# Two transformer layers on one core: score and maximum matmuls issued in runs of four heads, with all other TensorE work behind each run

## What is computed

```
x = x + xattn0(layernorm(x), ctx)      # causal self-attention ("s") plus cross-attention ("x"), added, one projection
x = x + ffn0(layernorm(x))             # 256 -> 1024 -> 256, ternary weights, 8-bit tokens, gelu
x = x + xattn1(layernorm(x), ctx, ctx) # cross-attention ("f")
x = x + ffn1(layernorm(x))             # 8-bit with one scale for the whole tensor: needs a maximum over all batches
```

## Time and profile before

| | us |
|---|---|
| median of 3 runs | 1773.9 (1767.2 to 1776.56) |
| profiled execution | 1771.38 |
| its span, first to last instruction | 1769.6 |
| from the first score of the first unit to the start of the last unit, 95 units | 58.6 to 1643.5 |
| PE busy | 1542.9 (87%) |
| DVE, ACT, POOL busy | 1331.3 (75%), 1141.1 (64%), 464.1 (26%) |
| mean granted TensorE clock | 0.932 of full speed |

### The profile page before, as it was taken

How to read it: one execution, slowest core, us unless ns; L and a number is a source line. 1 busy time by engine, 2 the same in 40 slices (tenths; PEclk the granted TensorE clock), 3 DMA queues, 4 the chain that set the end, 5 groups by cost and what they waited for, 6 DMA issues and landing times.

```text
span 1769.6 us, 31233 instructions
## 1 busy us (share of the span) xinstructions
PE 1542.9 (87%) x11094; PEld 664.2 (38%) x11094; DVE 1331.3 (75%) x2583; ACT 1141.1 (64%) x2178; POOL 464.1 (26%) x677
## 2 busy tenths in 40 slices
PE   3998889988999989988998899988988987898677
PEld 1244334423443235423542344323543442232226
DVE  6787765888678777888688876888488687778287
ACT  1374575667856675676765685667655854866497
POOL 3211412330324122331333132422341232310130
PEclk9798979999999989999999999999999898789899
DMA  6322201212121212121121212121221121011313
GB/s 185 98 85 85 87 19 34 73 46 67 34 73 49 70 40 67 53 62 57 34 74 41 63 47 67 52 70 56 56 63 33 29 64 31 25 59 39 143 60 120
DMA packets 115018, 110.99 MB, mean 63 GB/s; under 512 B 21552, under 2 KB 108720, under 8 KB 114864
## 3 DMA queue, kind: packets, MB, share of 16 engines
q1 hardware_dynamic: 114864, 108.99, 20.8%
HBM read 69.35 MB, written 38.80 MB: 61 GB/s over the span
## 4 chain that ended last, share of the span: by engine, by line
PE 52%; DVE 23%; ACT 12%; issue 4%; POOL 4%; DMA 3%; SPq 2%; ACTq 0%; POOLq 0%; DVEq 0%
PE acc L1628 13%; DVE nmax L1367 12%; PE st L1614 10%; PE misc L1558 8%; PE misc L1530 5%; ACT probs L1048 4%; PE misc L1584 4%; PE misc L1655 3%; PE misc L1570 3%; ACT tail_h L1118 2%; DVE hid L1316 2%; PE misc L1595 2%; PE misc L1682 2%; DMA stack<-nrow 2%; ACT tail_h L1103 1%
## 5 line engine op out<-in xcount | busy, mean ns | idle before, releaser
L1367 DVE TENSOR_REDUCE nmax<-misc 128x1 f32<-128x512 f32 (+3 forms) x1408 | 863.5, 660 | 261.4 <-PE misc L1584 128.7
L1048 ACT ACTIVATE probs<-st 128x512 f32<-128x512 f32 (+3 forms) x1536 | 756.1, 546 | 323.8 <-PE st L1614 205.4
L1584 PE MATMUL misc<-stack 48*128 48x512 f16 (+3 forms) x1536 | 484.0, 372 | 45.2 <-DVE nmax L1367 37.5
L1614 PE MATMUL st<-stack 50*128 50x512 f16 (+3 forms) x1536 | 472.9, 372 | 56.3 <-ACT probs L1048 43.8
L1614 PEld LDWEIGHTS st<-stack 50*128 50x128 f16 x1536 | 119.4, 94 | 503.2 <-ACT probs L1048 294.0
L1584 PEld LDWEIGHTS misc<-stack 48*128 48x128 f16 x1536 | 129.1, 94 | 117.2 <-DVE nmax L1367 86.8
L1628 PE MATMUL acc<-probs,v_x 128*32 128x512 f32 x1152 | 172.8, 675 | 0.0
L927 POOL TENSOR_TENSOR parts<-qk,zero 128x512 f16<-128x512 f32 x78 | 81.1, 1040 | 295.4 <-ACT qk L1034 295.3
L1034 ACT ACTIVATE qk<-misc,b 128x512 f32<-128x512 f32 x96 | 66.0, 687 | 137.6 <-PE misc L1558 137.3
L1628 PE MATMUL acc<-probs,v_s 128*32 128x512 f32 (+3 forms) x1152 | 115.8, 474 | 0.1
L1628 PE MATMUL acc<-probs,v_f 128*32 128x512 f32 x768 | 107.3, 632 | 0.0
(11 more groups left out here) (282 smaller groups left out, 2088.7 us busy)
## 6 DMA issues: line engine op xcount, KB each, us to landing
parts_xk<-parts SPq DMA_DIRECT2D x36, 128.0 KB
parts_xq<-parts SPq DMA_DIRECT2D x36, 128.0 KB
stack<-parts_xq SPq DMA_DIRECT2D x72, 64.0 KB, 2.1
stack<-parts_xk SPq DMA_DIRECT2D x72, 64.0 KB, 2.0
xn_A<-in_x_dram SPq DMA_DIRECT2D x8, 512.0 KB, 4.4
hid<-in_L_ffn_w_dram SPq DMA_DIRECT2D x4, 1024.0 KB, 5.4
parts_sk<-parts SPq DMA_DIRECT2D x32, 128.0 KB
parts_sq<-parts SPq DMA_DIRECT2D x32, 128.0 KB
```

Source lines behind the costliest of these rows:

```text
L1048: act.activation(probs[:, j % P_SLOTS, c, T - w:], st_bank(n, 4 * j + c)[:, 0:w], ACT.Exp, scale=scale_of[s.unit[1]]).then_inc(exp_done, 1)
L1367: dve.tensor_reduce(nmax[:, ring, first:first + NT * (len(cs) - 1) + 1:NT], src, AX.X, ALU.max, negate=True).then_inc(misc_free[slot], 1)
L1584: last = pe.matmul(o, stack[rows, r, 0, c // 2, P * i:P * i + P], stack[rows, r, 1, c // 2, 0:w], start=True, stop=not causal)
L1614: last = pe.matmul(o[:, 0:w], stack[rows, r, 1, c // 2, P * j:P * j + P], stack[rows, r, 0, c // 2, T - w:T], start=True, stop=not causal)
```

## The change

A constant `RUN = 4` groups the places. Since a block has four heads, each block becomes one run: the four pairs follow one another, then `values` (and in block 0 `heads_copy`), then `heads_out` (block 1), `negmax_T` (block 2) or `negmax` (block 0), and then the other steps of all four places in one piece. No instruction is added or removed, and buffers, banks and semaphores are as before. Only the order in the list differs.

```diff
+RUN = 4
     for j in range(NT):
-        for c in range(HU):
-            out.append(("scores", u, j, c))
-            out += maxima[HU * j + c]
-            if c == 3 and j:
+        for c in range(0, HU, RUN):
+            for d in range(c, c + RUN):
+                out.append(("scores", u, j, d))
+                out += maxima[HU * j + d]
+            last_run = c + RUN == HU
+            if last_run and j:
                 out.append(("values", u, j - 1))
-            if (j, c) == (0, 3) and prev:
+            if last_run and j == 0 and prev:
                 out += [("values", prev, NT - 1), ("heads_copy", prev)]
-            if (j, c) == (1, 1) and prev:
+            if c == 0 and j == 1 and prev:
                 out.append(("heads_out", prev))
-            if (j, c) == (0, 2) and next_:
+            if c == 0 and j == 2 and next_:
+                out.append(("negmax_T", next_))
+            if last_run and j == 0 and next_:
                 out.append(("negmax", next_))
-            if (j, c) == (2, 0) and next_:
-                out.append(("negmax_T", next_))
-            out += others[HU * j + c]
+            for d in range(c, c + RUN):
+                out += others[HU * j + d]
```

## The result

| | before | after |
|---|---|---|
| median of 4 runs, us | 1775.23 (1767.2 to 1778.37) | 1897.81 (1894.36 to 1905.75) |
| profiled execution, us | 1771.38 | 1905.75 |
| its span, us | 1769.6 | 1903.9 |
| mean granted TensorE clock | 0.932 | 0.891 |

The ratio is 1.0688 [1.0656, 1.072]: the kernel is slower, by 122.6 us where 49 were forecast, and the time lies 12 us above the stated range (1749 to 1886). Lines are five higher than before (L1614 is now L1619, L1584 is L1589, L1602 is L1607).

The account below looks back on a forecast made before the run. PE's order was taken to bound most stretches (52% of the chain, DVE 23%). Terms -52 + 85 + 10 + 10 + 10 = +63 us, times 0.77 = 49, turned 1771.4 into 1820 us; eight in ten, 1749 to 1886.

Parts of the forecast that it names:

- The faster rival: Fourth score's wait falls where PE would wait for DVE or ACT anyway: 1749 us, chance 0.17.
- The fourth score's wait: Fourth score waits for ACT's exp to free a bank: 0.45 us in 150 full-width blocks, 0.2 in 91 others, +85 us.
- Copies out late: ACT's copies from the block's last step delay the next run's first exp: +10 us, bounds 0 and 20.
- The next unit's maxima: `negmax_T` comes 2.1 us later, its DMA delaying the next unit's first score: +10 us, bounds 0 and 76.
- maxima late in most tight units: Rival: SP is free, so 2.1 us come through in all 36 cases, +76 instead of +10: 1886 us, chance 0.15.
- No clock term: TensorE clock given no cost, since it stayed at 1.00 in a stretch full of such waits.
- the factor 0.77: DVE has 23% of the chain, where a later PE costs nothing: 63 x 0.77 = 49 us.
- the prediction's own sum before the factor: All five terms where PE sets the pace: -52 + 85 + 10 + 10 + 10 = +63 us.
- the 52 us: Net gain on PE: 71 us of removed switches less 19 us of added changes behind the values.
- the pairs' 0.23 us, the 0.32 to the values: On PE, pairs start 0.23 us apart; values start 0.32 us after the last pair.
- the switches' gain: 354 excursions between 64-row and 128-row work leave PE's order, 0.2 us each: 71 us.
- dependent steps side by side: Where `norm_T` and `v`, or `heads_out` and `y_T`, lose the work between them: +10 us, bounds 0 and 20.

Follow-up runs that it names:

- the square: Changed kernel (1.0688), with `negmax_T` directly behind block 1's values (1.0442), with values ahead of the fourth pair (1.0306), with both (1.0049).
- run3_values_pair: Changed kernel with the values between the third and fourth pair, `negmax_T` still late: 1836.4 us, 1.0306.
- run4_turn_values: Changed kernel, runs of four kept, with `negmax_T` directly behind the values of block 1: 1860.67 us, 1.0442.
- run3_turn_early: Changed kernel with values between the third and fourth pair and `negmax_T` directly behind block 1's values: 1788.13 us, 1.0049.

## Why the prediction went wrong

**Direction and place: right.** The fourth score waits for the exp, as forecast, 1.14 us after the first, and the ratio falls by 0.038 where the wait is taken out. The faster rival (waits hidden) is out.

**The term "The fourth score's wait", +85, was too small.** The rows give 95.5 us more wait (139.3 - 43.8). Each wait is about 0.13 us longer than its row says: in the clean block the fourth score starts 0.45 us later than at 0.69, and the row has 0.32. With 178 cases more this makes 95.5 + 23 = 119 us, by an estimate from these rows. The count was not too low (241 blocks were assumed, 178 came) but the length was: the mean is 139.3 / 265 = 0.53 us where the clean block has 0.32. The clean block is typical, the median being 0.34; it is 31 waits of over 1 us that hold 51 of the 139 us. "Copies out late" had its usual case right (behind a projection alone, in 80 blocks, the exp starts 0.69 us after the score) and missed the blocks with more in ACT's queue. In the changed kernel's timeline, a block that follows a projection and `quant_T`, PE and ACT:

```profile
629.70 0.69 ACT L1039 ACTIVATE qk<-misc,b 128x512 f32<-128x512 f32 x1 [2.31 <-PE misc L1563]
...
630.04 0.39 PE L1619 MATMUL st<-stack 50*128 50x512 f16 x1
...
630.28 1.07 ACT L1007 COPY hqT<-misc 128x512 bf16<-128x512 bf16 x2
...
631.23 2.09 ACT L1053 ACTIVATE probs<-st 128x512 f32<-128x512 f32 x4
...
631.90 0.39 PE L1619 MATMUL st<-stack 50*128 50x512 f16 x1 [0.60 <-ACT probs L1053]
```

Three copies of the block stand in ACT's queue ahead of the first exp, which starts 1.19 us after its score, not 0.69, and the fourth score comes 1.86 us after the first. Worse is an ACT step that waits itself:

```profile
1335.66 1.24 ACT L1088 ACTIVATE hid<-hid,magic,tok_hq 128x1024 f32<-128x1024 f32 x1 [2.82 <-DVE tok_hq L1297]
1336.80 1.55 ACT L1053 ACTIVATE probs<-st 128x512 f32<-128x512 f32 x3
```

```profile
1337.43 0.61 PE L1619 MATMUL st<-stack 50*128 50x512 f16 x1 [3.57 <-ACT probs L1053]
```

ACT waits 2.82 us for DVE in the other steps; the exps are behind it, and PE, behind them, stands 3.57 us.

**The term "The next unit's maxima", +10 of a range to 76, was too small.** It costs 44 and 46 us in the two pairs of the square. The rival "maxima late in most tight units" was right in kind: the weight loads' wait grew by 45.3 - 25.8 = 19.5 us. A second wait was not foreseen. `negmax_T` takes a `misc` bank, and behind four maxima in a row this is a bank that DVE hasn't read yet. Timeline of DVE and PE in the changed kernel:

```profile
459.77 1.37 DVE L1284 TENSOR_SCALAR xn_C<-x,mv_E,rstd_E 128x256 f32<-128x256 f32 x4
...
461.18 1.22 DVE L1405 TENSOR_REDUCE xpeak<-xn_C 128x1 f32<-128x1024 f32 x1
...
462.51 2.48 DVE L1372 TENSOR_REDUCE nmax<-misc 128x1 f32<-128x512 f32 x4
...
463.30 0.26 PE L1607 MATMUL misc<-identh,nparts 128*32 128x128 f16 x1 [2.72 <-issue]
```

DVE finishes other work, then reduces the four maxima; one takes 2.48 / 4 = 0.62 us, so the first is done at 463.13 and `negmax_T` starts 0.17 us later. The profile names no releaser ("issue"), but the order of the two engines does. Before, the row had 0.5 us in all; now 26.8.

**"No clock term" was wrong.** The clock moved by 0.041 between the profiled executions, twice the 0.02 that the prediction named as its own disproof, and by over 0.02 between any two executions of the two kernels. With two levels, 1.2 and 2.4 GHz, time at half speed is twice the missing share of the span: 2 x 0.068 x 1769.6 = 241 us before, 2 x 0.109 x 1903.9 = 415 after. The stretch of the earlier trace rows that stayed at 1.00 has short waits; the changed kernel has longer ones, 31 of over 1 us for an exp where there were 9. Its windows around the wait shown above (length; busy PE, PEld, DVE, ACT, POOL; clock):

```profile
1326.00:1333.70 7.70, 6.71 (x61) 2.70 (x60) 5.22 (x9) 5.43 (x12) 2.49 (x4) 1.00 0.46 168
1333.70:1337.40 3.70, 0.17 (x4) 0.02 (x1) 1.46 (x7) 1.74 (x3) 1.35 (x2) 0.79 0.41 117
1337.40:1342.00 4.60, 4.57 (x27) 1.77 (x27) 0.72 (x2) 2.73 (x5) 2.08 (x4) 0.50 0.19 52
```

```profile
1338.72 1.93 PE L1633 MATMUL acc<-probs,v_x 128*32 128x512 f32 x8
```

PE runs at 2.4 GHz (1.00) up to 1333.7, is idle for nearly 3.7 us, in which the clock falls, and then works 4.6 us at 1.2 GHz (0.50) with hardly a gap. The next values take 1.93 us instead of 1.07. The earlier `negmax_T` gave back 0.016 of the clock in the profiled executions of both pairs of the square; taking out the exps' wait gave back none (0.891 to 0.889).

What the clock cost can be estimated from the same traces. PE's time is the sum of its steps, each from one matmul's start to the next. Each pair of neighbouring instructions has a median step at full clock and without a wait (over the eleven kernels here without fillers or other banks). The sum of these medians depends on the order alone. What a step takes beyond its median is put down to a wait (PE idle for over 0.15 us before the second start), to the clock (both starts at half speed, no wait) or to the rest (steps across a change of the clock, and scatter). One profiled execution each, differences in us, rounded:

| from, to | order | waits | clock | rest | span |
|---|---|---|---|---|---|
| before, changed | -68 | +131 | +69 | +2 | +134 |
| changed, values in front (`run3_values_pair`) | +52 | -129 | +9 | +2 | -67 |
| changed, `negmax_T` early (`run4_turn_values`) | -5 | -15 | -22 | -3 | -45 |
| values in front, both (`run3_turn_early`) | -16 | -10 | -24 | +1 | -49 |
| before, both (`run3_turn_early`) | -32 | -8 | +53 | +6 | +18 |

With means in place of medians the clock has 58 instead of 69 us in the first line and 45 instead of 53 in the last, and the first line has -69 for the order and +128 for the waits. This is an account, an estimate from one trace against another, and not a test: no run changes the clock alone.

**The steps that failed are "No clock term" and the factor 0.77.** Order and waits come to +63 us (+59 by means), which is the prediction's own sum before the factor. So by this account PE lost the whole of it, and the factor took away 14 us that did come. Another 58 to 69 us are the slower matmuls, which had no term. That the sum before the factor fits is luck: the fourth score's wait was 34 us longer than its term and the maxima later, but the order gave more than the 52 us, and the maxima's own wait for DVE (-30) and the wait for `heads` (15.6 to 0.7 us), which became smaller, had no term. The late `negmax_T` costs through the clock as well: about half of the 45 and 49 us that an earlier one saves stands in that column.

The Trainium skill's page "TensorE: Matmul & The Clock Gate", section "HAM oscillation — how this bites in real kernels", prices half-speed time at half its length: by an estimate from that figure, 174 us more would be 87. The account has 58 to 69 for these 174 us. For `run3_turn_early`, with 2 x 0.095 x 1787.8 = 340 us at half speed, 99 more than before, it has 45 to 53, which is about half; fewer switches, on the other side of the account, leave 18 us between the two profiled executions.

**Right in size:** the pairs' 0.23 us, the 0.32 to the values, the exp after a plain projection, and the switches as far as the account shows them. There the 300 excursions that `run3_values_pair` adds cost 52 us, 0.17 us each, where 0.2 were read. **Open:** the switches' gain in a run of its own, and dependent steps side by side (+10), which was not tried alone.

## What to carry to other kernels

Before bundling alike matmuls, count the buffers that a whole run takes from each ring, on both sides of a pair: a run longer than the ring turns saved switches (0.1 us each way here) into a wait for the consumer (0.53 us in the mean here), and moving a bank from one ring to the other here only moved the wait. Look at what comes to stand behind the run as well: one small step that starts a chain over several engines (transpose, copy, DMA, next unit) cost about 45 us by being some two microseconds late, and it is cheap to place it by itself. Then follow the chain to its last queue: placed a little earlier, the step only waited in SP's. A wait read in a clean stretch gave the median and missed the few long ones, which held more than a third of the time and came with the lower clock. So ask what an order does to the longest waits, and don't put the clock at nothing because one stretch kept it.

## What the runs showed of the hardware

- In the place shown, a stall of nearly 3.7 us on PE is followed by 4.6 us of nearly unbroken work at half clock: the stall is paid for again after it ended. Over the whole kernel such slow steps come to 58 to 69 us more than before, by the account above.
- PE's idle time in the rows is too short where its matmuls overlap: 0.32 us stood for 0.45 us between starts.
- Moving one of seven PSUM banks from the general ring to the scores cost the kernel before 3.0% by itself (1.0303); the tail, whose banks were split another way, took 119.6 us from the last score on instead of 117.4.
